# A transformer block on one core: sequence 0 in another order, ternary weights in one form, dense key-value sums

## The chip, the cores and the metric

The kernel runs on one core of a Trainium2 chip. A core has five engines that run their own instruction streams side by side: TensorE (matrix products, PE in the profile, its weight loads PEld), VectorE (DVE), ScalarE (ACT), GpSimd (POOL) and SyncE (SP, which here issues DMAs). The metric is the device time of one execution in microseconds.

## The reference

Sixteen sequences of 512 tokens with 512 features go through one pre-norm block: mLSTM attention of eight heads, then a feed-forward with ternary weights.

```python
def _mlstm_scan(q, k, v, i_pre, f_pre):          # per head, over the 512 tokens
    f_log = jax.nn.log_sigmoid(f_t)
    m_new = jnp.maximum(f_log + m, i_t)
    F = jnp.exp(f_log + m - m_new)
    I = jnp.exp(i_t - m_new)
    C_new = F[..., None, None] * C + (I[..., None] * k_t)[..., :, None] * v_t[..., None, :]
    n_new = F[..., None] * n + I[..., None] * k_t
    h_num = jnp.einsum('bhd,bhdv->bhv', qs, C_new)
    qn = jnp.einsum('bhd,bhd->bh', qs, n_new)
    h = h_num / (jnp.maximum(jnp.abs(qn), jnp.exp(-m_new)) + EPS)[..., None]

def _L0_attn_ref(x, ...):                        # q, k: 8 heads of 32; v: 8 heads of 64
    i_pre = soft_cap(x @ Wig.T + big)
    f_pre = soft_cap(x @ Wfg.T + bfg)
    h_norm = _multihead_norm(h, gamma)           # per head, over its 64 numbers
    y = (jax.nn.sigmoid(x @ Wog.T) * h_norm) @ Wout.T

def absmean_quant(w):
    scale = jnp.mean(jnp.abs(w))
    return jnp.sign(w) * (jnp.abs(w) >= scale * 0.7)

def _L0_ffn_ref(x, w1, b1, w2, b2):              # 512 -> 2048 -> 512
    h = jax.nn.gelu(x @ absmean_quant(w1).T + b1, approximate=False)
    return h @ absmean_quant(w2).T + b2

x = x + _L0_attn_ref(_layernorm(x), ...)
x = x + _L0_ffn_ref(_layernorm(x), ...)
```

## The kernel before

**Precision.** A product of two f32 matrices is made in f16 with both split into a high and a low part: high by high, low by high and high by low, three matmuls of 128 x 512 for each 128 rows of the contraction. The ternary weights are exact in f16 and need two (high and low of the activations). Small f32 products (scores times values, transposes, the state) are f32 matmuls.

**Attention by chunks.** A sequence is cut into four chunks of 128 tokens. `scores(b, g)` makes query-key products for four heads at a time, `weigh(b, n)` on VectorE multiplies those of head n with its decays (`dec`). A chunk's result is the sum of two things in the same PSUM bank: what earlier chunks left in the state, `chunk_state`, and the weighed scores times the values with a column of ones (64 + 1 = 65 columns a head), `chunk_head`. Two groups of four heads, of 32 query features each, fill the 128 rows of a product. The state before a chunk is built in two steps. `outer(b, j)` makes the key-value sum of chunk j per head, eight products of 65 columns into 32 rows of `ph`, and `state(b, j)` on VectorE adds it to the decayed previous one, densely in the free half of `kT`. Then `spread_state` on GpSimd writes it out to `cst` as a block-diagonal matrix of 4 x 65 = 260 columns (multiplied with `own_head`, a mask of each head's 32 rows), so that `chunk_state` can treat four heads in one f32 product of 128 rows and 260 columns, two products a chunk. `head_stats` on VectorE reads a chunk's result, takes its mean per head, and squares (ScalarE), a power (GpSimd) and the gate follow.

**PSUM.** There are eight banks of 512 f32 columns, in pairs: `pa` (projections and half of the scores), `pf` (feed-forward), `ps` (key transposes, the other half of the scores), `ph` (values 2 and 3, gate columns, key-value sums, chunk results). A use of a bank waits for the release of its previous use; in `pa` the uses are numbered (`U_GATE` to `U_Y`).

**Order.** No scheduler orders the work: each engine runs a program written out by hand, with semaphores between them. For sequences 1 to 15 the attention of sequence b and the feed-forward of sequence b - 1 (`fb`) are interleaved: on TensorE `hidden(...)` are first-layer tiles, `model(...)` second-layer ones, and each chunk's eight head products have one second-layer matmul between each two. After sequence 15 its feed-forward runs alone. The normalised next inputs are prepared in the same pass.

**Sequence 0** has no feed-forward beside it. In its place all weights are made ready. Five matrices are read in f32: the gates' and `Wv` first, then `Wq` with `Wk`, `Wog`, `Wout`. TensorE transposes them (`weights`), four tiles into one bank of `wbank`, ScalarE writes the high part (`weights_hi`) and VectorE the low part (`weights_lo`). `wbank` has four banks (both of `ps`, both of `pf`), used in turn. The maxima of the weights (`maxima`) are needed for scaling; `w1` and `w2` are summed in magnitude on ScalarE (`absolute_sums1`, `absolute_sums2`), `weight_sums` adds over the partitions and `thresholds` makes the ternary bounds. `w1` and `w2` are 16 units of 128 x 512 each. The units of `w1` become ternary by a comparison on GpSimd (even units) or VectorE (odd ones) and a second operation on VectorE for each; TensorE transposes two units with eight f16 transposes into one bank, and ScalarE copies 128 x 1024 out. The units of `w2` go by pairs in another form: ScalarE makes two signs of the even unit, VectorE two operations of the odd one, TensorE twelve small matmuls with the identity into two banks, ScalarE two sign copies. The `w1` pairs lie between the heads of `scores` and `weigh`; those of `w2` come through `between(...)`, between the key-value sums, the chunks and the projections of the result (`project`), after each of which VectorE has a `residual`.

Two places of the hand-written order, from TensorE's program (L1799) and from VectorE's:

```python
                key_tokens_first(b)
                for n in range(T):
                    tokens(b, U_O + n, xT[:, :, n, :, :], C_O)
                    if first and n == 1:
                        weight_sums()
                key_tokens_last(b)
                outer(b, 0)
```
```python
                between(4)
                between(5)
                residual(b, 0, ca)
                between(6)
                residual(b, 1, ca)
```

## Time and profile before

| what | value |
|---|---|
| time, median of 3 runs | 1897.43 us (1897.35 to 1898.04) |
| the profiled execution: its time / its span | 1898.05 us / 1896.3 us |
| TensorE busy | 1829.0 us, 96% |
| VectorE busy | 1231.2 us, 65% |
| ScalarE busy | 1034.1 us, 55% |
| GpSimd busy | 625.7 us, 33% |
| mean granted TensorE clock | 0.98 of full speed |

The span is what the profiler saw from the first instruction to the last; the execution's own time is 1.75 us longer. A busy share is an average over stages with different limits, so the sections below read single stretches. The clock stands as a share of 2.4 GHz: 1.00 is that level, 0.50 is 1.2 GHz, and a value between is a mix over the stretch. In the timeline a group of pipelined matmuls shows the time to the end of its last one, so neighbours overlap; distances between starts are exact.

### The profile page before, as it was taken

The page shows a single profiled execution, that of the slowest core. Times are in us where ns is not written, and L with a number is a line of the kernel's source. Part 1 is how long each engine was busy: PE and PEld are TensorE (multiplying, and loading weights), DVE is VectorE, ACT ScalarE, POOL GpSimd, SP SyncE. Part 2 cuts the span into 40 slices and gives each one's busy share as a digit, 9 for nine tenths or more (in the row PEclk, how much of TensorE's full clock was granted, in tenths as well). Part 3 has the DMA queues.
Part 4 walks back from the last instruction along what each step waited for, and adds up shares of the span by engine and source line. Part 5 has one row for each costly group of instructions (what it writes and reads, how often), then busy time and mean ns, then how long its engine had stood idle before and what let it go on. Part 6 is the DMA issues. An engine that isn't in the chain of part 4 may idle for free.

```text
span 1896.3 us, 28994 instructions
## 1 busy us (share of the span) xinstructions
PE 1829.0 (96%) x11260; PEld 966.7 (51%) x11260; DVE 1231.2 (65%) x2259; ACT 1034.1 (55%) x1711; POOL 625.7 (33%) x447
## 2 busy tenths in 40 slices
PE   5779999999999999999999999999999999999989
PEld 3364544545455464645546464554645455464544
DVE  6877575675767667575765757576575756746542
ACT  6657647274563727456372745737275473736523
POOL 1534133433414343241434324143432324333230
PEclk8769999999999999999999999999999999999989
DMA  7423224251422425042251513325141432413010
GB/s 276 161 80 96 57 71 111 51 137 25 113 51 54 134 49 139 23 115 51 51 137 45 134 32 104 62 51 137 45 124 35 103 71 51 115 42 102 12 40 22
DMA packets 233512, 156.78 MB, mean 83 GB/s; under 512 B 195088, under 2 KB 199312, under 8 KB 228256
## 3 DMA queue, kind: packets, MB, share of 16 engines
q1 hardware_dynamic: 231792, 151.79, 31.2%
q10 hardware_dynamic: 1584, 3.15, 0.5%
q8 instruction: 89, 1.46, 0.3%
q14 instruction: 47, 0.39, 0.1%
HBM read 90.48 MB, written 17.24 MB: 57 GB/s over the span
## 4 chain that ended last, share of the span: by engine, by line
PE 76%; DVE 11%; ACT 7%; issue 2%; DMA 0%; POOL 0%; SPq 0%; POOLq 0%; DVEq 0%; ACTq 0%
PE pf L1736 23%; PE pf L1722 21%; PE pa L1612 17%; PE pa L1594 5%; PE ph L1695 4%; ACT dec L855 2%; PE ph L1689 2%; ACT L875 1%; DVE g L1188 1%; DVE g L1186 1%; DVE mean L1115 1%; ACT gT L758 1%; DVE xres L1332 1%; PE ps L1671 1%; PE ph L1653 1%
## 5 line engine op out<-in xcount | busy, mean ns | idle before, releaser
L1736 PE MATMUL pf<-w2T,gT 128*128 128x512 f16 x2048 | 535.2, 379 | 0.0
L1722 PE MATMUL pf<-x2T,w1T 128*128 128x512 f16 x2048 | 457.4, 381 | 3.4 <-ACT g L875 2.8
L1348 DVE SCALAR_TENSOR_TENSOR gT<-g,wscale,gT 128x512 f16<-128x512 f32 x256 | 192.1, 750 | 205.6 <-ACT gT L878 204.2
L1722 PEld LDWEIGHTS pf<-x2T,w1T 128*128 128x128 f16 x2048 | 194.5, 98 | 237.7 <-ACT g L875 5.9
L1736 PEld LDWEIGHTS pf<-w2T,gT 128*128 128x128 f16 x2048 | 224.4, 111 | 173.8
L1612 PE MATMUL pa<-wT,xT 128*128 128x512 f16 x1152 | 256.3, 381 | 1.9 <-DVE qT L1164 1.2
L568 POOL TENSOR_TENSOR dec<-dec,causal 128x1024 f32<-128x1024 f32 x64 | 170.2, 2690 | 248.1 <-DMA dec<-gate_r 248.1
L875 ACT ACTIVATE g<-pf,b1c 128x512 f32<-128x512 f32 x256 | 175.7, 686 | 86.8 <-PE pf L1722 86.6
L883 ACT ACTIVATE ktok<-kT 128x512 f32<-128x512 f32 x64 | 40.3, 630 | 325.6 <-DVE kT L1286 325.6
L1695 PEld LDWEIGHTS ph<-vaug,dec 128*128 128x128 f32 x1024 | 184.4, 195 | 19.9
L878 ACT ACTIVATE gT<-g,wscale 128x512 f16<-128x512 f32 x256 | 184.8, 722 | 8.4
L583 POOL TENSOR_TENSOR cst<-kT,own_head 128x520 f32<-128x520 f32 x48 | 51.5, 1073 | 408.2 <-DVE kT L1242 227.1
L1612 PEld LDWEIGHTS pa<-wT,xT 128*128 128x128 f16 x1152 | 111.8, 98 | 136.4 <-DVE qT L1164 5.8
L1594 PE MATMUL pa<-xT,wT 128*128 128x512 f16 x768 | 173.0, 382 | 7.5 <-ACT kT L833 6.6
L1612 PE MATMUL pa<-wT,hoT 128*128 128x512 f16 x768 | 176.1, 383 | 0.0
L1695 PE MATMUL ph<-vaug,dec 128*128 128x65 f32 x1024 | 170.1, 253 | 0.0
L590 POOL TENSOR_TENSOR hinv<-hvar,half 128x8 f32<-128x8 f32 x64 | 105.1, 1643 | 165.3 <-DVE hvar L1299 165.3
L855 ACT ACTIVATE dec<-dec,gtok 128x128 f32<-128x128 f32 x512 | 155.8, 390 | 1.4 <-POOL dec L568 1.1
L597 POOL TENSOR_TENSOR qT<-kT,qT 128x512 f16<-128x512 f32 x64 | 74.3, 1161 | 206.5 <-ACT qT L890 206.5
L1277 DVE TENSOR_TENSOR den<-ph,gtok 128x8 f32<-128x8 f32 x64 | 10.6, 166 | 175.1 <-PE ph L1695 175.1
L1594 PEld LDWEIGHTS pa<-xT,wT 128*128 128x128 f16 x768 | 74.3, 98 | 97.2 <-ACT kT L833 8.4
L1612 PEld LDWEIGHTS pa<-wT,hoT 128*128 128x128 f16 x768 | 75.8, 99 | 91.4 <-issue 3.0
(211 smaller groups left out, 2358.4 us busy)
## 6 DMA issues: line engine op xcount, KB each, us to landing
dec<-gate_r SPq DMA_DIRECT2D x32, 1024.0 KB, 6.4
xin<-L_attn_x SPq DMA_DIRECT2D x16, 1024.0 KB, 6.1
out<-x1b SPq DMA_DIRECT2D x64, 256.0 KB, 2.2
xres<-L_attn_x SPq DMA_DIRECT2D x16, 512.0 KB, 6.1
xres<-L_attn_x SPq DMA_DIRECT2D x32, 256.0 KB, 3.6
qw<-gate_w SPq DMA_DIRECT2D x128, 48.0 KB, 5.9
gT<-L_ffn_w SPq DMA_DIRECT2D x5, 1024.0 KB, 4.9
gT<-L_ffn_w ACTq DMA_DIRECT2D x3, 1024.0 KB, 5.6
```

What stands on the lines that cost most here:

```text
L568: nc.gpsimd.tensor_tensor(rows_of, rows_of, causal[:, :].unsqueeze(1).to_broadcast([P, 2 * T, P]), ALU.add).then_inc(masked, 1)
L590: nc.gpsimd.tensor_tensor(hinv[:, :], hvar[:, :], half[:, :], ALU.pow).then_inc(pool_a, 1)
L597: nc.gpsimd.tensor_tensor(head_parts[j % 2][:, LO, :], cent[j % 2], head_parts[j % 2][:, HI, :], ALU.subtract).then_inc(ho_lo[j], 1)
L855: last = nc.scalar.activation(dec[:, h, tok(j)], dec[:, h, tok(j)], ACT.Exp, bias=gtok[:, j, ROW_C, h:h + 1])
L875: nc.scalar.activation(g32[:, f % 2, :], pf[:, use % 2, :], ACT.Gelu, bias=b1c[:, f:f + 1], scale=1.0 / X_SCALE).then_inc(pf_free[use % 2], 1)
L878: nc.scalar.activation(gT[:, HI, f, :], g32[:, f % 2, :], ACT.Copy, scale=wscale[:, W_GELU:W_GELU + 1]).then_inc(g_hi, 1)
L1348: nc.vector.scalar_tensor_tensor(gT[:, LO, f, :], g32[:, f % 2, :], wscale[:, W_GELU:W_GELU + 1], gT[:, HI, f, :], ALU.mult, ALU.subtract) ...
L1594: last = nc.tensor.matmul(bank, wT[:, ws, k, col:col + P], xT[:, xs, :, k, :], start=(k == 0 and n == 0), stop=(k == KD - 1 and n == 2))
L1612: last = nc.tensor.matmul(bank, src[:, xs, k, :], wT[:, ws, k, col:col + D], start=(k == 0 and n == 0), stop=(k == KD - 1 and n == 2))
L1695: last = nc.tensor.matmul(ph[:, g, i * VA:(i + 1) * VA], dec[:, h, tok(j)], vaug[:, j, h, :], start=(j == 0 and i == 0), stop=(i == H4 - 1 ...
L1722: last = nc.tensor.matmul(bank, w1T[:, k, tok(f)], x2T[:, part, :, k, :], start=(k == 0 and part == HI), stop=(k == KD - 1 and part == LO))
L1736: last = nc.tensor.matmul(bank, gT[:, part, f, tok(t)], w2T[:, f, :], start=(f == 0 and part == HI), stop=(f == NF - 1 and part == LO), sk ...
```

## The change

**Key-value sums and state.** `cst` holds the state densely (65 columns a group of heads), and `state` writes it there. `spread_state`, `own_head` and the semaphore between them are gone. `chunk_state` makes one product a head, of the head's 32 rows and 65 columns, and head i of either group writes into bank i, so four heads lie on four row groups and in four banks. `ps` and `ph` become two halves of one PSUM tensor `psh` of four banks. `chunk_head` writes the same banks, `head_stats` reads all four.

**Keys, values, gates, decays.** The values of tile 1 go to `ps` in place of `pa`; the last key transpose (`U_KLAST`) is gone from `pa`, all six key transposes stand together ahead of the output gates; the gate rows `gi`, `gf` lie in `sig`, no longer in `kT`. On ScalarE the evacuation of key tile 0 stands ahead of the last gate exponentials, and the last decays ahead of the output gates 2 and 3.

**Sequence 0.** The second `maxima` stand ahead of the values. `wbank` has six entries of which the query, key and output-gate weights use three in turn and `Wout` the two of `pa`. Attention up to chunk 0 comes first; sums, thresholds and all 16 pairs of ternary units follow it, all in the form that `w2` had. GpSimd has no part in them. VectorE makes pairs 11 and 12 behind residual 0, 13 and 14 behind residual 1, 15 behind residual 2, where the pairs up to 6 of 7 stood ahead of residual 1. SyncE's loads of `w2` stand between the head outputs.

```diff
-    U_GATE, U_V, U_K, U_Q, U_O, U_KLAST = 0, 1, 3, 5, 7, 11
-    U_S = U_KLAST + 1
+    U_GATE, U_V, U_K, U_Q, U_O, U_S = 0, 1, 2, 4, 6, 10
...
-        cst = sb("cst", [P, T - 1, HG, H4 * VA])
+        cst = sb("cst", [P, T - 1, HG, VA])
...
-        gi, gf = kT[0:NH, 0, :], kT[0:NH, 1, :]
+        gi, gf = sig[0:NH, 0, :], sig[0:NH, 1, :]
...
-        pa, pf, ps, ph = pb("pa"), pb("pf"), pb("ps"), pb("ph")
+        pa, pf = pb("pa"), pb("pf")
+        psh = ctx.enter_context(nc.psum_tensor("psh", [P, H4, 512], F32))
+        ps, ph = psh[:, 0:2, :], psh[:, 2:4, :]
...
-        wbank = [ps[:, 0, :], ps[:, 1, :], pf[:, 0, :], pf[:, 1, :]]
+        wbank = [ps[:, 0, :], pf[:, 0, :], pf[:, 1, :], ps[:, 1, :], pa[:, 0, :], pa[:, 1, :]]
...
-            return n % 2 if n in USES_OUT else n % 4
+            if n in USES_OUT:
+                return 4 + (n - USES_OUT[0]) % 2
+            return n if n in USES_V else (n - USE_GATE) % 3
...
-            def spread_state(b, j):
...
+            def signs(*pairs):
+
+                for p in pairs:
+                    m, q = matrix(p)
+                    act.wait_ge(s_w12[m][q // 2], 16)
+                    if p == 0:
+                        act.wait_ge(s_thr, 1)
+                    if p >= 2:
+                        act.wait_ge(s_ufill, p - 1)
+                    nc.scalar.activation(tern(2 * q), rows[:, 2 * q, :], ACT.Sign, bias=nthr[:, m:m + 1])
+                    nc.scalar.activation(low(2 * q), rows[:, 2 * q, :], ACT.Sign, bias=thr[:, m:m + 1]).then_inc(s_sign, 1)
...
                 if fb is not None:
                     tokens2_hi(fb, HALVES[0])
+                    keys(b, 0)
                 act.wait_ge(gate_dve, at(b, 4, 4))
...
-            def ternary(*units):
...
+            def ternary(*pairs):
+
+                for p in pairs:
+                    m, q = matrix(p)
+                    u = 2 * q + 1
+                    dve.wait_ge(s_w12[m][q // 2], 16)
+                    if p >= 2:
+                        dve.wait_ge(s_ufill, p - 1)
+                    nc.vector.tensor_scalar(low(u), rows[:, u, :], nthr[:, m:m + 1], None, ALU.is_le).then_inc(s_low, 1)
+                    dve.wait_ge(s_low, p + 1)
+                    nc.vector.scalar_tensor_tensor(tern(u), rows[:, u, :], thr[:, m:m + 1], low(u), ALU.is_ge,
                                                    ALU.subtract).then_inc(s_tern, 1)
...
                 if j > 0:
-                    pe.wait_ge(c_ok, at(b, T - 1, j))
                     for g in range(HG):
-                        nc.tensor.matmul(ph[:, g, 0:H4 * VA], qw[:, g, tok(j - 1)], cst[:, j - 1, g, :],
-                                         start=True, stop=False, skip_group_check=True)
+                        for h in range(H4):
+                            own = slice(h * DQ, (h + 1) * DQ)
+                            nc.tensor.matmul(psh[:, h, g * VA:(g + 1) * VA], qw[own, g, tok(j - 1)], cst[own, j - 1, g, :],
+                                             start=(g == 0), stop=False, skip_group_check=True)
...
-                last = nc.tensor.matmul(ph[:, g, i * VA:(i + 1) * VA], dec[:, h, tok(j)], vaug[:, j, h, :],
-                                        start=(j == 0 and i == 0), stop=(i == H4 - 1), skip_group_check=True)
+                last = nc.tensor.matmul(psh[:, i, g * VA:(g + 1) * VA], dec[:, h, tok(j)], vaug[:, j, h, :],
+                                        start=(j == 0 and g == 0), stop=(g == HG - 1), skip_group_check=True)
```

TensorE's program for sequence 0 is now, in calls: scores of both groups, `outer` 1 and 2, chunk 0, `weight_sums`, pairs 0 and 1, chunk 1, pairs 2 and 3, two tiles of `Wout`, chunk 2, pairs 4 and 5, the next input's first half, two tiles of `Wout`, chunk 3, pairs 6 and 7, the next input's second half, pairs 8 to 10, project 0, pairs 11 and 12, project 1, pairs 13 and 14, project 2, pair 15, project 3.

Three places in the order of instructions. **TensorE, sequence 0, values and weight transposes.** `L1497` (after: `L1462`) are weight transposes, `L1612` (`L1576`) the values, `L1594` (`L1552`) the first key product, `L1510` and `L1512` (`L1475`, `L1477`) the maxima. Before:

```order
L1497 MATMUL ps<-ident,gT 128x128 x4
L1497 MATMUL pf<-ident,gT 128x128 x4
L1612 MATMUL pa<-wT,xT 128x512 x12
L1510 MATMUL ph<-ident,peak 5x128
L1512 MATMUL ph<-cst 128x5
L1497 MATMUL pf<-ident,gT 128x128 x4
L1612 MATMUL pa<-wT,xT 128x512 x12
L1497 MATMUL ps<-ident,gT 128x128 x4
L1612 MATMUL ph<-wT,xT 128x512 x24
L1497 MATMUL ps<-ident,gT 128x128 x4
L1497 MATMUL pf<-ident,gT 128x128 x4
L1594 MATMUL pa<-xT,wT 128x512 x12
```

After:

```order
L1475 MATMUL psh<-ident,peak 5x128
L1477 MATMUL psh<-cst 128x5
L1462 MATMUL pf<-ident,gT 128x128 x8
L1576 MATMUL pa<-wT,xT 128x512 x12
L1462 MATMUL psh<-ident,gT 128x128 x4
L1576 MATMUL psh<-wT,xT 128x512 x12
L1462 MATMUL pf<-ident,gT 128x128 x4
L1576 MATMUL psh<-wT,xT 128x512 x24
L1462 MATMUL pf<-ident,gT 128x128 x4
L1462 MATMUL psh<-ident,gT 128x128 x4
L1552 MATMUL pa<-xT,wT 128x512 x12
```

The maxima moved ahead of the values. The last query-key tile (the lone `pf` row between the second and the last two values) goes into the bank of the first, behind which the last 24 value products stand.

**VectorE, the end of sequence 0.** `L1104` and `L1106` (after: `L1076`, `L1078`) make one odd ternary unit, `L1318` and `L1321` (`L1286`, `L1289`) are a residual and its statistics, `L1109` is the next input's normalisation. Before:

```order
L1104 TENSOR_SCALAR x2T<-gT,w 128x512
L1106 SCALAR_TENSOR_TENSOR x2T<-gT,w,x2T 128x512
L1104 TENSOR_SCALAR x2T<-gT,w 128x512
L1106 SCALAR_TENSOR_TENSOR x2T<-gT,w,x2T 128x512
L1318 SCALAR_TENSOR_TENSOR xres<-pa,evac,xres 128x512
L1321 BN_STATS stats<-xres 128x6
L1104 TENSOR_SCALAR x2T<-gT,w 128x512
L1106 SCALAR_TENSOR_TENSOR x2T<-gT,w,x2T 128x512
L1318 SCALAR_TENSOR_TENSOR xres<-pa,evac,xres 128x512
L1321 BN_STATS stats<-xres 128x6
```

After:

```order
L1286 SCALAR_TENSOR_TENSOR xres<-pa,evac,xres 128x512
L1289 BN_STATS stats<-xres 128x6
L1076 TENSOR_SCALAR x2T<-gT,w 128x512
L1078 SCALAR_TENSOR_TENSOR x2T<-gT,w,x2T 128x512
L1076 TENSOR_SCALAR x2T<-gT,w 128x512
L1078 SCALAR_TENSOR_TENSOR x2T<-gT,w,x2T 128x512
L1286 SCALAR_TENSOR_TENSOR xres<-pa,evac,xres 128x512
L1289 BN_STATS stats<-xres 128x6
L1109 TENSOR_SCALAR xin<-xin,mean,rstd 128x512 x4
L1076 TENSOR_SCALAR x2T<-gT,w 128x512
L1078 SCALAR_TENSOR_TENSOR x2T<-gT,w,x2T 128x512
```

Two units stand between the first residual and the second, where one stood, and five units in all are left behind the first residual, where two were.

**TensorE, a chunk of a later sequence.** `L1689` (after: `L1654`) is the state product, `L1695` (`L1660`) a head product, `L1736` (`L1701`) the second feed-forward layer. Before:

```order
L1736 MATMUL pf<-w2T,gT 128x512 x16
L1689 MATMUL ph<-cst,qw 128x260 x2
L1736 MATMUL pf<-w2T,gT 128x512
L1695 MATMUL ph<-vaug,dec 128x65
L1736 MATMUL pf<-w2T,gT 128x512
```

After:

```order
L1701 MATMUL pf<-w2T,gT 128x512 x16
L1654 MATMUL psh<-cst,qw 128x65 x8
L1701 MATMUL pf<-w2T,gT 128x512
L1660 MATMUL psh<-vaug,dec 128x65
L1701 MATMUL pf<-w2T,gT 128x512
```

Eight products of 65 columns stand where two of 260 stood; what surrounds them keeps its order.

## Rows read from the trace of the kernel before

**Rows 1.** Busy time by stretch: length, busy (instructions) by engine, TensorE clock, DMA share, GB/s.
```profile
0.00:153.00 153.00, 104.91 (x698) 68.46 (x699) 114.28 (x228) 95.66 (x161) 56.67 (x57) 0.79 0.49 163
75.00:100.00 25.00, 10.64 (x176) 8.18 (x176) 23.25 (x33) 10.30 (x16) 11.89 (x7) 0.57 0.45 143
264.00:376.00 112.00, 111.30 (x690) 58.30 (x689) 74.14 (x136) 60.99 (x101) 37.95 (x26) 1.00 0.30 80
94.00:153.00 59.00, 43.79 (x300) 33.81 (x301) 45.32 (x96) 33.94 (x53) 23.05 (x18) 0.73 0.26 75
```
**Rows 2.** Timeline of TensorE, gate products: start, length, engine, line, operation, tiles, count.
```profile
153.12 1.89 PE L1585 MATMUL pa<-xT,wgT 128*128 128x512 f16 x8
...
264.00 1.89 PE L1585 MATMUL pa<-xT,wgT 128*128 128x512 f16 x8
...
375.48 1.89 PE L1585 MATMUL pa<-xT,wgT 128*128 128x512 f16 x8
```
**Rows 3.** Waits of TensorE: what waited for whom, total us, times, longest.
```profile
PE pa L1594 <- ACT kT L833: 6.6, 13, 0.5
...
PE pf L1722 <- ACT g L875: 2.8, 15, 0.2
```
**Rows 4.** Timeline of ScalarE, sequence 0: decays, signs, sign copies.
```profile
65.01 2.43 ACT L855 ACTIVATE dec<-dec,gtok 128x128 f32<-128x128 f32 x8
...
99.47 0.71 ACT L727 ACTIVATE x2T<-gT,w 128x512 f16<-128x512 f32 x1
...
102.34 1.09 ACT L735 ACTIVATE w2T<-pf 128x512 f16<-128x512 f32 x2 [0.33 <-PE pf L1542]
```
**Rows 5.** Timeline of TensorE, sequence 1: a state product.
```profile
226.25 1.04 PE L1689 MATMUL ph<-cst,qw 128*128 128x260 f32 x4
227.12 0.38 PE L1736 MATMUL pf<-w2T,gT 128*128 128x512 f16 x1
```
**Rows 6.** Timeline of TensorE, sequence 3: transposes, key-value sums.
```profile
409.67 0.38 PE L1626 MATMUL pa<-ident,kT 128*128 128x128 f32 x2
409.99 0.43 PE L1653 MATMUL ph<-vaug,ktok 128*32 128x65 f32 x16
410.35 2.98 PE L1722 MATMUL pf<-x2T,w1T 128*128 128x512 f16 x13
```
**Rows 7.** Timeline of TensorE, sequence 0: eight head products of chunk 1.
```profile
112.91 1.90 PE L1695 MATMUL ph<-vaug,dec 128*128 128x65 f32 x16
114.65 0.22 PE L1540 MATMUL pf<-ident,x2T 128*128 128x128 f16 x1
```
**Rows 8.** Weight loads in groups: shapes, count, busy us, mean ns, idle before.
```profile
L1695 PEld LDWEIGHTS ph<-vaug,dec 128*128 128x128 f32 x1024 | 184.4, 195 | 19.9
...
L1671 PEld LDWEIGHTS ps<-hoT 32*128 32x128 f16 x768 | 22.0, 94 | 13.4 <-issue 13.4
```
**Rows 9.** Timeline of VectorE, sequence 0: gate chain, a ternary unit, a residual.
```profile
44.11 0.54 DVE L1202 TENSOR_TENSOR kT<-stack,qT 8x384 f32<-8x384 f32 x1
...
98.62 0.49 DVE L1104 TENSOR_SCALAR x2T<-gT,w 128x512 f16<-128x512 f32 x1 [0.54 <-PE pf L1530]
99.14 0.75 DVE L1106 SCALAR_TENSOR_TENSOR x2T<-gT,w,x2T 128x512 f16<-128x512 f32 x1
...
141.47 0.74 DVE L1318 SCALAR_TENSOR_TENSOR xres<-pa,evac,xres 128x512 f32<-128x512 f32 x1
```
**Rows 10.** Timeline of TensorE, sequence 0: keys, scores, projections, a ternary pair.
```profile
47.54 4.44 PE L1594 MATMUL pa<-xT,wT 128*128 128x512 f16 x12 [0.86 <-DVE wT L1067]
...
75.04 0.23 PE L1671 MATMUL ps<-hoT 32*128 32x128 f16 x2 [0.36 <-DVE ktok L1220]
...
130.64 3.88 PE L1612 MATMUL pa<-wT,hoT 128*128 128x512 f16 x12
...
144.50 0.22 PE L1540 MATMUL pf<-ident,x2T 128*128 128x128 f16 x1
...
145.17 2.75 PE L1612 MATMUL pa<-wT,hoT 128*128 128x512 f16 x12
```

521 lines of the change are left out of this document (248 added, 273 removed).

## The prediction

> **What bounds the kernel now.** I read the busy time by stage first. Where the feed-forward of one sequence runs beside attention of the next, TensorE is busy 111.30 of 112 us at the full clock, VectorE 74, ScalarE 61 [rows 1]: there only TensorE's work and its own short waits count. The gate product that opens a sequence starts at 153.12, 264.00 and 375.48 [rows 2]: a period of 110.88 or 111.48. The other stage is sequence 0, the first 153 us. TensorE is busy 105 of 153 there, at a mean granted clock of 0.79; VectorE 114, ScalarE 96 [rows 1]. That is a chain of engines that wait for each other, and its length is what has to be worked out. The feed-forward tail is untouched. So the change is two sums: 15 periods, and one prologue.
>
> **Later sequences.** (a) The wait at the second query or key product. TensorE waits 6.6 us in 13 places for a key evacuation (L833), and 2.8 us in 15 places for a gelu (L875) [rows 3]. After, the first key tile's evacuation stands ahead of the last gate exponentials on ScalarE, and the gate rows lie in `sig`, no longer in `kT`, so neither key evacuation waits for them. The periods with and without this wait differ by 0.60 us; 13 x 0.60 = 7.8. The gelu wait sits after the first scores, and the last decay pair stood between the output-gate copies and gelu in both orders; now the copies come last, 0.6 us each behind a decay that VectorE's work doesn't need before them. By my count gelu starts about 1 us earlier, since the idle time between copy and decays closes: 2.8 more. Sum (a) -10.6. If the copies of output gates 2 and 3 became late, the first scores would wait; they are needed 3.6 us (16 products) after the last one's product, and the exponentials in front of them take 2.4 [rows 4]. Cover enough, by about 1 us.
>
> (b) The state products. Before, two products of 260 columns take 226.25 to 227.12 = 0.87 us [rows 5], three times a sequence, 45 times in all. Each streams 217 ns twice. After, eight products of 32 rows x 65 columns, four of them on separate row groups and separate banks. The nearest rows: the key-value sums (L1653), eight products of 65 columns on four column groups. From 409.67 to 410.35, less two transposes of 0.11 each, they cost 0.46 us with the way into the tiled form and out of it [rows 6]. That is the low end. But their weights are 32 columns; the new ones load 128 columns in f32. Such loads are what the head products of sequence 0 wait for: 16 of them in 112.91 to 114.65, 109 ns each, though 65 columns stream in 54 (a quarter of 217) [rows 7]. Four rounds at 109 rather than 57 ns add 0.21: 0.67 us. I take 0.67, since the form of the load, not of the stream, is what it is nearest to: gain 0.20, x 45 = -9. At the low end -18. At the high end the four groups' loads come one after another, 16 x 0.109 + 0.2 = 1.94 us: +48. Loads of 32 rows take 94 ns in f16, those of 128 x 128 in f32 195 [rows 8]; the rows do not say whether four at once share a path.
>
> The Trainium skill (TensorE: Matmul & The Clock Gate, "LDWEIGHTS") says that a 32 x 128 load takes as long as a 128 x 128 one, as only columns count. It speaks against this change: K is cut to a quarter and the load stays. By it and row tiles that load side by side the sum is the 0.67 above; with whole-array streams hiding no load it would never reach 0.46. The TensorEngine Tiling page ("Key Properties") says that different tiles can load and multiply in parallel, which would rule out the high end. No run here shows it for f32 loads of row tiles.
>
> (c) Nothing else is on TensorE's path. Two transposes move ahead of the output gates, at the same price. GpSimd loses 48 spreads of 1.07 us, VectorE's head sums read four banks, the same 512 numbers: both engines have a third of each period or more free [rows 1]. I cost these at nothing; what covers them are the feed-forward's products between a chunk and the next. If VectorE's sums took longer from four banks by more than that, the next chunk would wait, three times a period.
> Sum for the later sequences: -10.6 - 9 = -20 (from -29; +38 with serial loads).
>
> **Sequence 0.** I strung each engine's new order with durations of before. The same list strung in the order of before ends at 152 where the trace has 153.1, so it may be 1 us short.
> 1. Early weights. The magnitudes now come ahead of the values, so VectorE's gate chain, which ended at 44.65 (44.11 + 0.54, [rows 9]), ends about 2.9 earlier, at 41.8. But only three banks now take the weight transposes, and the fourth query-key tile needs the low part of the first, which VectorE makes behind the gate chain, at 42.5. Values 2 and 3 are queued behind it on TensorE, ScalarE has their copies and an exponential to do before that tile's high part, and the keys wait for it. The first key product starts near 52.3, not 47.54 [rows 10]: +4.8. Of this ScalarE gives some back, since five of its absolute sums now stand behind the decays: first decay 67.0 (before 65.01, [rows 4]); four groups of 2.43 and four copies later, 78.9, the first scores: 79 (before 75.04, [rows 10]): +4.
> 2. To the thresholds. Before, the ternary work of w1 ran inside scores and decays. After: eight weighings, of the form of the residual's operation at 0.74 [rows 9], with the first scores before and the second between them, to about 88; second and third sums, 90; chunk 0 at half the clock, twice 1.74 = 3.5 [rows 7]; the sum product, some 0.8: thresholds at 94. That moves the work of eight pairs from before 94 to behind it.
> 3. Chunks. From 94 to its end, before had 45.3 us of VectorE and 33.9 of ScalarE in 59 [rows 1]. A pair of tiles now takes ScalarE two signs of 0.71 and two copies in 1.09 [rows 4], 2.2 with the 0.1 by which neighbours overlap, and VectorE 0.49 + 0.75 = 1.24 [rows 9]. Eight more pairs give ScalarE 33.9 + 17.6 = 51.5, less two copies of 1.0 of the first matrix that fell behind 94 before: 49.5. They give VectorE 45.3 + 9.9, less some 5 of weighings and ternary that fell there: 50. So neither is done before 144, if they never waited for each other. They do: heads 0 on VectorE at 96.6, sigmoid until 102.4, transposes 1 to 105, chunk 1 until 107.8, heads 1 until 109.8, output weights at 114, chunk 2 until 119, next x at 121 to 124.5, chunk 3 until 129, pair 8 at 136, pairs 9 and 10 to 145.
> 4. The end. The projection of tile 0 starts at 145 (before 130.6), and from here each step waits for the one before: VectorE makes pairs 11 and 12 only behind residual 0, which waits for projection 0, and TensorE needs pair 11 before projection 1. One round: projection 2.6 at the full clock (145.17 row, [rows 10]) to 5.2 at half; residual 1.5 with its statistics (0.74 the first of them); ternary 1.24; twelve small matmuls 0.7 (144.50 to 145.17, [rows 10]) to 1.4; copies 1.1; twelve more, 1.4; = 8.6 to 11.8. I have projection 1 at 156.5, projection 2 at 168.2 (a normalisation lies between), projection 3 at 175.6, the gates of sequence 1 at 178.
> Before, pairs stood one ahead of the residual and the whole end took 153.1 - 130.6 = 22.5 us from projection 0. So sequence 0 ends 25 us later: 178 against 153. With the clock full throughout the same list gives 166 (+13), at half 194 (+41); the granted clock was 0.57 from 75 to 100, with TensorE busy 10.6 of 25, and 1.00 where it is busy throughout [rows 1]. I let it rise in the list only behind solid stretches of products; with those instants shifted the list gave 173 to 181.
>
> **Sum.** 1898.05 (the profiled execution's own time) + 25 - 20 = 1903; it lies 0.6 above the median of the runs, so 1902.5 on that scale.
>
> **The rivals.**
> Cheap tiles, short prologue. The state products cost 0.46 and the clock stays up in half of the ternary stretch: +18 - 29 = -11, 1887. For it: the key-value sums did run four abreast. Against: the f32 load price.
> Low clock. TensorE is less than half busy from 94 on, and from 75 to 100, busy as little, it had 0.57 [rows 1]. With the list near half clock to its end, +38 - 20 = +18, 1916.
> Serial loads. Row groups share the load path: +25 + 38 = +63, 1960. It decides from 0.87 us a chunk upwards; the pace of sixteen f32 loads is the test.
> The prologue comes out even: if ScalarE and VectorE ran ahead as before, it would end near 158 and leave -15: 1882. Against it stands VectorE's order of residuals and ternary pairs, which is fixed in the code.
>
> **How the numbers follow.** My forecast 0.50; cheap tiles 0.20; low clock 0.15; serial loads 0.08; even prologue 0.07. Predicted 1902.5. The forecast's own range is 1894 to 1912. For 8 in 10 the range takes the cheap tiles at the low end and the low clock's centre: 1885 to 1917, which leaves out the serial loads, half of the even prologue and the far side of the low clock. A measurement of this kernel tells 0.2% (3.8 us) from no change. Faster than 1893.6: 0.27 from the two faster rivals, less what of them lies above, 0.24. Slower than 1901.2: 0.30 of the forecast, and 0.23 of the two slower ones: 0.50, leaving 0.26 for the same.
>
> **What would show it.** The period between gate products: 109.9 to 110.5 (111.48 before); under 109.6 means tiles at the low end, over 111.5 serial loads. The eight state products at 0.67 us with their ways in and out; no wait for a key evacuation left at the second query or key product. In sequence 0: thresholds at 94, projection 0 near 145, gates of sequence 1 near 178, VectorE's waits for projections between ternary pairs. I am wrong at the root if the gates of sequence 1 start before 165, or if a new wait at the scores or the keys shows in the later periods.

## The result

The changed kernel is slower. Its five runs gave a median of 1921.88 us (1913.13 to 1926.24), those of the kernel before 1898.04 (1897.35 to 1899.26): a ratio of 1.0122, with a 95% interval of 1.0108 to 1.0135, or 24 us. Forecast were 1902.5 and a range up to 1917. The direction was right, the size too small by 19 us, and the median lies outside the range; of the five runs only the fastest lies inside.

The profiled execution of after was its fastest, 1913.13 us with a span of 1911.3, so 15.0 longer than the span of before. Two questions follow. Where do these 15 us come from? And why do the other executions take 8 to 13 us more, when those of before differ by 2?

The first view is again the timeline of TensorE with the gate products that open sequences 1 to 4 (start, length, engine, line, operation, tiles, count); it answers to [rows 2]:

```profile
185.86 1.46 PE L1543 MATMUL pa<-xT,wgT 128*128 128x512 f16 x6
...
295.90 1.46 PE L1543 MATMUL pa<-xT,wgT 128*128 128x512 f16 x6
...
408.34 1.89 PE L1543 MATMUL pa<-xT,wgT 128*128 128x512 f16 x8
...
518.37 1.89 PE L1543 MATMUL pa<-xT,wgT 128*128 128x512 f16 x8
```

Sequence 0 ends at 185.86, not 153.12: 32.7 us later. The periods are then 110.04, 112.44 and 110.03. Twelve of the fourteen between gate products are 110.03; two, those of sequences 2 and 9, are 112.44 and 112.11. From the gates of sequence 1 to the end after needs 1911.3 - 185.86 = 1725.4, before 1896.3 - 153.12 = 1743.2: 17.7 less. So 32.7 - 17.7 = 15.0. Forecast were +25 and -20, together +5: of the 10 us by which this execution misses the forecast, 7.7 lie in sequence 0 and 2.3 behind it.

By stage, after (busy time by engine, clock last but two; compare [rows 1]):

```profile
0.00:186.00 186.00, 114.32 (x767) 75.46 (x768) 108.36 (x220) 106.33 (x185) 40.40 (x43) 0.74 0.40 134
94.00:145.00 51.00, 29.01 (x245) 26.22 (x246) 33.82 (x71) 35.13 (x58) 15.76 (x12) 0.63 0.44 136
145.00:186.00 41.00, 24.43 (x127) 13.29 (x126) 15.95 (x31) 15.71 (x26) 4.95 (x4) 0.71 0.04 12
410.00:522.00 112.00, 112.00 (x733) 57.96 (x731) 76.15 (x144) 61.56 (x102) 38.02 (x24) 1.00 0.33 80
```

From the page of after, busy time and share (before: 1829.0, 1231.2, 1034.1 and 625.7):

```profile
PE 1825.2 (95%) x11868; PEld 958.9 (50%) x11868; DVE 1228.3 (64%) x2251; ACT 1044.6 (55%) x1735; POOL 590.0 (31%) x388
```

The busy times hardly moved, but for GpSimd's, which lost the spreads and is not the bottleneck; so the 15 us are waits and clock. In the last 41 us of sequence 0 no engine is busy for more than 60% of the time: VectorE 16, ScalarE 16, TensorE 24 at a clock of 0.71. That is a chain of waits. The later sequences have no idle time left on TensorE (112.00 of 112).

### The profile page after: what moved, and what is told of

Same layout as the page of the kernel before. It is cut to its first block, busy times and chain, and to the rows that moved or that the text cites. A ratio compares the mean times of both kernels' runs of the same rounds, so it can differ in the third digit from the quotient of the medians.

```text
span 1911.3 us, 30148 instructions
## 1 busy us (share of the span) xinstructions
PE 1825.2 (95%) x11868; PEld 958.9 (50%) x11868; DVE 1228.3 (64%) x2251; ACT 1044.6 (55%) x1735; POOL 590.0 (31%) x388
## 3 DMA queue, kind: packets, MB, share of 16 engines
q10 hardware_dynamic: 1584, 3.15, 0.5%
## 4 chain that ended last, share of the span: by engine, by line
PE 89%; ACT 2%; issue 1%; POOL 1%; DVE 1%; DMA 1%; POOLq 0%; SPq 0%; DVEq 0%; ACTq 0%
PE pf L1701 23%; PE pf L1687 23%; PE pa L1576 18%; PE pa L1552 7%; PE psh L1576 6%; PE psh L1660 5%; PE psh L1654 2%; PE pa L1543 1%; POOL dec L565 1%; PE psh L1635 1%; PE psh L1617 1%; DMA dec<-gate_r 1%; PE psh L1590 0%; PE pf L1498 0%; ACT dec L839 0%
## 5 line engine op out<-in xcount | busy, mean ns | idle before, releaser
L1701 PE MATMUL pf<-w2T,gT 128*128 128x512 f16 x2048 | 535.7, 379 | 0.0
L1701 PEld LDWEIGHTS pf<-w2T,gT 128*128 128x128 f16 x2048 | 224.2, 111 | 175.6
L565 POOL TENSOR_TENSOR dec<-dec,causal 128x1024 f32<-128x1024 f32 x64 | 175.6, 2775 | 249.0 <-DMA dec<-gate_r 249.0
L1576 PE MATMUL pa<-wT,xT 128*128 128x512 f16 x960 | 213.2, 380 | 0.0
L1660 PEld LDWEIGHTS psh<-vaug,dec 128*128 128x128 f32 x1024 | 186.1, 197 | 15.3 <-DVE cst L1220 0.8
L1576 PE MATMUL pa<-wT,hoT 128*128 128x512 f16 x768 | 179.4, 388 | 0.0
L1660 PE MATMUL psh<-vaug,dec 128*128 128x65 f32 x1024 | 172.2, 256 | 0.6 <-DVE cst L1220 0.6
L1552 PE MATMUL pa<-xT,wT 128*128 128x512 f16 x768 | 171.2, 379 | 1.0 <-DVE wT L1056 1.0
L839 ACT ACTIVATE dec<-dec,gtok 128x128 f32<-128x128 f32 x512 | 154.9, 391 | 6.5 <-POOL dec L565 6.0
L1576 PEld LDWEIGHTS pa<-wT,xT 128*128 128x128 f16 x960 | 94.2, 98 | 110.0 <-issue 1.0
L1576 PE MATMUL psh<-wT,xT 128*128 128x512 f16 x576 | 129.4, 384 | 0.0
L1576 PEld LDWEIGHTS pa<-wT,hoT 128*128 128x128 f16 x768 | 76.7, 100 | 93.8 <-issue 7.3
L595 POOL TENSOR_TENSOR x1b<-xres,b2r 128x512 f32<-128x512 f32 x64 | 81.3, 1271 | 132.0 <-DVE xres L1286 95.9
L1552 PEld LDWEIGHTS pa<-xT,wT 128*128 128x128 f16 x768 | 74.4, 98 | 87.7 <-DVE wT L1056 1.2
```

The source lines that it names most:

```text
L565: nc.gpsimd.tensor_tensor(rows_of, rows_of, causal[:, :].unsqueeze(1).to_broadcast([P, 2 * T, P]), ALU.add).then_inc(masked, 1)
L595: nc.gpsimd.tensor_tensor(x1b[:, t, :], xres[:, t, :], b2r[:, :], ALU.add).then_inc(x1b_ok, 1)
L839: last = nc.scalar.activation(dec[:, h, tok(j)], dec[:, h, tok(j)], ACT.Exp, bias=gtok[:, j, ROW_C, h:h + 1])
L1552: last = nc.tensor.matmul(bank, wT[:, ws, k, col:col + P], xT[:, xs, :, k, :], start=(k == 0 and n == 0), stop=(k == KD - 1 and n == 2))
L1576: last = nc.tensor.matmul(bank, src[:, xs, k, :], wT[:, ws, k, col:col + D], start=(k == 0 and n == 0), stop=(k == KD - 1 and n == 2))
L1660: last = nc.tensor.matmul(psh[:, i, g * VA:(g + 1) * VA], dec[:, h, tok(j)], vaug[:, j, h, :], start=(j == 0 and g == 0), stop=(g == HG - ...
```

## What a later sequence gained

A state product of sequence 3, the row that answers to [rows 5]:

```profile
481.21 0.67 PE L1654 MATMUL psh<-cst,qw 32*128 32x65 f32 x16
481.82 0.39 PE L1701 MATMUL pf<-w2T,gT 128*128 128x512 f16 x1
```

Eight products take 0.61 us with their ways in and out, where two took 0.87. (Each f32 product stands in the trace as two records, so x16 are eight products.) The waits of TensorE over the whole program (us, times, longest) no longer hold one for a key evacuation; they hold these:

```profile
PE psh L1635 <- ACT sig L799: 4.7, 3, 2.4
...
PE pf L1687 <- ACT g L859: 2.3, 3, 0.9
```

The first of these is new: the first scores wait for a copy of an output gate. One of the three times, of 2.4 us, is in sequence 0; the later sequences have two, 2.3 us together. The prediction had named this wait and called the cover enough; it had also put down a new wait at the scores of the later periods as a sign that it is wrong at the root.

**Experiment: the state products twice.** It tells what four products abreast cost.

```diff
-                    for g in range(HG):
+                    for g in (0, 1, 0, 1):
                         for h in range(H4):
                             own = slice(h * DQ, (h + 1) * DQ)
```

> The changed kernel with the eight state products of a chunk issued twice (the second pass overwrites the first, so nothing else changes): 24 products more a sequence. From the profile of after, eight take 0.61 us with their ways in and out (481.21 to 481.82). If row tiles load side by side at 109 ns a round of four, eight more products are four more rounds, 0.44 us, and the period goes up 3 x 0.44 = 1.3, to 111.35. If loads come one after another and only the first was hidden: 0.61 or more each, 1.8 to 5 a period. If they are free beside the stream (54 ns a round): 0.65 a period.

Measured, two gate products of sequences 3 and 4, and one doubled state product with its successor:

```profile
414.46 1.89 PE L1543 MATMUL pa<-xT,wgT 128*128 128x512 f16 x8
...
525.84 1.89 PE L1543 MATMUL pa<-xT,wgT 128*128 128x512 f16 x8
```
```profile
487.34 1.12 PE L1654 MATMUL psh<-cst,qw 32*128 32x65 f32 x32
488.39 0.39 PE L1701 MATMUL pf<-w2T,gT 128*128 128x512 f16 x1
```

One run, 1943.35 us. The period is 111.37 in the most, 1.34 more than 110.03: 0.45 us for eight products, and 488.39 - 487.34 = 1.05 against 0.61, 0.44 more. That is four rounds of 110 ns, since 16 more records come in fours. The single records show the fours: weight loads of the doubled product start at 487.445, 487.452, 487.459 and 487.465, the next four at 487.554 to 487.574. So four f32 row tiles of 32 rows load side by side, 7 ns apart, and a round goes at the pace of one f32 load, the 109 ns of [rows 7], not at that of its 65 columns, 54 ns. Both the serial loads and the 0.46 of the key-value sums are out. The run as a whole is longer than after by more than 15 x 1.34, for two reasons beside the products: its gates of sequence 1 come at 191.72, and it has two long periods, of 113.85 and 115.28.

**Experiment: the key evacuation back behind the last gate exponentials.**

```diff
                     tokens2_hi(fb, HALVES[0])
-                    keys(b, 0)
...
-                    keys(b, 1)
+                    keys(b, 0, 1)
```

> The changed kernel with the evacuation of key tile 0 back behind the last gate exponentials in the later sequences; the gate rows stay where they are. If it was the place on ScalarE that removed the wait at the second query or key product, that wait comes back, 0.4 to 0.6 us in most sequences, and the periods are 110.5 to 110.6. If it was the gate rows' move out of the key tile, the period stays at 110.03.

Two gate products, of sequences 5 and 6, and the wait:

```profile
627.79 1.89 PE L1542 MATMUL pa<-xT,wgT 128*128 128x512 f16 x8
...
738.54 1.89 PE L1542 MATMUL pa<-xT,wgT 128*128 128x512 f16 x8
```
```profile
PE pa L1551 <- ACT kT L816: 5.9, 11, 0.6
```

One run, 1921.03 us. The wait is back in 11 places for 5.9 us, as the 6.6 in 13 places of [rows 3], and most periods are 110.74. Four are 110.08, as before had two without the wait. So the move of the gate rows out of the key tile does not remove the wait by itself; the place on ScalarE does. (Whether that place would do with the rows still in the key tile was not run.) Its price in a period is 0.66 to 0.71, somewhat over the wait itself.

## The late copies

**Why two periods are 2.1 to 2.4 longer.** ScalarE's timeline in sequence 2 (long) and in sequence 3 (normal), decays `L839`, copies `L799`:

```profile
326.74 2.44 ACT L839 ACTIVATE dec<-dec,gtok 128x128 f32<-128x128 f32 x8
331.17 2.44 ACT L839 ACTIVATE dec<-dec,gtok 128x128 f32<-128x128 f32 x8 [1.99 <-POOL dec L565]
333.52 1.24 ACT L799 ACTIVATE sig<-pa,evac 128x512 f32<-128x512 f32 x2
...
437.98 4.77 ACT L839 ACTIVATE dec<-dec,gtok 128x128 f32<-128x128 f32 x16
442.64 1.25 ACT L799 ACTIVATE sig<-pa,evac 128x512 f32<-128x512 f32 x2
```

In the long one ScalarE stands 1.99 us in front of the last decays, since GpSimd masks those (`L565`) late, and the two copies are queued behind. They start at 333.52 - 295.90 = 37.6 us of the sequence, against 34.3, and the first scores, which need their banks, wait:

```profile
335.02 0.23 PE L1635 MATMUL psh<-hoT 32*128 32x128 f16 x2 [1.31 <-ACT sig L799]
```

Before had such late masks too. In ScalarE's waits of before:

```profile
ACT dec L855 <- POOL dec L568: 1.1, 2, 0.7
```

They fell on sequences 4 and 13, whose periods are 111.49 and 111.48 like the rest: there the copies stood ahead of the decays, and nothing came of it.

**Experiment: the changed kernel once more**, for a second profile.

> The changed kernel once more, unaltered, for a second profile. Its runs spread from 1913.1 to 1926.2 us where those of before spread by 1.9. Theory A, late copies: in each later sequence in which GpSimd masks the last decays late, the two last output-gate copies come late on ScalarE and the first scores wait some 2.2 us; runs differ by how many sequences are hit (2 of 15 in the first profile, period 112.1 to 112.4 beside 110.03). A profile of an execution near 1920 then has some 6 such periods and the gates of sequence 1 near 186. Theory B, clock: runs differ in how low the clock stays in sequence 0; such a profile has its gates of sequence 1 near 194 and 2 long periods again.

Measured: 1918.81 us median (1916.54 to 1923.27); the profile had a span of 1915.7. Its gates of sequence 1 are at 186.3, and three periods are long, those of sequences 2, 9 and 13 (112.2, 112.3, 112.4). So long periods differ in number from one execution to the next, two here and three there, and in this execution the third is 2.3 of the 4.4 us; 0.4 more are in sequence 0 and 1.7 behind the gates of sequence 15. But neither theory is settled: the profile fell on an execution of 1917, with three long periods where theory A wanted six near 1920, and with its gates at 186 where theory B wanted 194.

**Experiment: both copies back ahead of the last decays.**

```diff
                 decay(b, 4)
-                decay(b, 6)
                 output_gate(b, 2, 3)
+                decay(b, 6)
```

> The changed kernel with the last two output-gate copies back ahead of the decays of heads 6 and 7 on ScalarE, in all sequences. Theory A: no period of 112 left, 15 periods of 110.0 to 110.1, the wait of the first scores for a copy gone, the runs within 2 us of each other as those of before, median about 1911.3 - 4.5 + 1.8 = 1908.6, less up to 2 in sequence 0. Theory B: the spread stays at some 10 us and the median stays above 1915. A third way: gelu starts later by the decays of two heads and the period rises to 110.2 or 110.5.

Measured: 1920.96 us (1919.33 to 1921.94), a ratio of 1.0116 (1.0099 to 1.0132) to before. The spread fell to 2.6 us, but theory A's time, 1908.6, was missed by 12: gelu pays, as the third way had it, and the gates of sequence 1 come at 187.98. The periods are 110.51, and the late masks (sequences 9 and 13) give 111.57 and 111.07. The waits for gelu:

```profile
PE pf L1687 <- ACT g L859: 8.1, 16, 1.5
```
```profile
440.96 0.67 ACT L799 ACTIVATE sig<-pa,evac 128x512 f32<-128x512 f32 x1
442.90 0.69 ACT L799 ACTIVATE sig<-pa,evac 128x512 f32<-128x512 f32 x1 [1.27 <-PE pa L1576]
443.49 2.43 ACT L839 ACTIVATE dec<-dec,gtok 128x128 f32<-128x128 f32 x8
```

ScalarE idles 1.27 us for the last product and only then turns to the decays. So beside the other steps this one gives 110.51 - 110.03 = 0.48 us in each sequence, 7 in all, and takes 2.1 to 2.4 in each with a late mask, where the old order loses 0.6 to 1.1.

A late mask can cost more than that. The kernels of the section on sequence 0 below keep this order of copies and decays, and they have periods of 113.8 to 114.5 beside such of 112.0 to 112.6. In both kinds the first mask starts 22.0 to 22.7 us into the sequence, against 20.6 to 21.4 elsewhere. In one of 114.45 (sequence 9 of the run with the fourth query-key tile behind the values) the stretch behind the wait reads (stretch, length, busy by engine, clock):

```profile
1105.00:1110.00 5.00, 4.08 (x31) 1.61 (x20) 2.50 (x4) 3.86 (x7) 0.00 (x0) 0.68 1.06 181
```

TensorE waited 1.7 us there for the copy and 0.9 for gelu, and its clock, 1.00 before, fell. Of thirteen long periods looked at in six traces, the clock fell behind the wait in all seven of +3.8 to +4.4 us and stayed at 1.00 in all six of +2.1 to +2.5, among them both of after. So such a wait costs 2 us when the clock holds and 4 when it falls. How many of the slower executions of after had such a fall was not seen.

**Experiment: copy 2, decay 6, copy 3, decay 7.**

> The changed kernel with ScalarE's order copy 2, decay of head 6, copy 3, decay of head 7 (all sequences). In the profile of after the last product of the output gates ends 33.8 us into a sequence and the first scores follow at 37.8; where the mask of heads 6 and 7 comes late (its start at 30.5 to 30.8 of the sequence, not 28.4) copy 3 starts at 38 and the scores wait. Theory: copy 3 now starts near 34 in a normal sequence and near 35.5 in a late one, gelu stays within 0.3 of its place; so all periods are 110.0 to 110.1 and no 112 is left, against 110.5 with both copies ahead: 1911.3 - 4.5 + 1.8 = 1908.6, and 1908 to 1916 with the clock of sequence 0. Rival: gelu slips by a copy's 0.6 us and periods are 110.3 or more.

Measured: 1915.11 us (1912.68 to 1917.78), 1.0092 (1.0077 to 1.0107) to before. Normal periods are 110.03, so the gain is kept; but three are still 111.8 to 112.0. The expectation that no long one is left was wrong. The median is 3.7 us below the second sample of after, 1918.81, and 6.8 below the first, 1921.88, near the spread of either. The waits say where the lateness went:

```profile
PE pf L1690 <- ACT g L860: 5.8, 4, 1.9
```

The scores no longer wait, the gelu behind them does, since it stands behind the same decays. In none of the three orders tried is the lateness of the mask hidden altogether; the order chooses what it hits.

## Where sequence 0 lost its time

The end of sequence 0 in after, TensorE (L1498 are a ternary pair's products, L1576 a projection), then VectorE. It answers to [rows 10]:

```profile
149.19 3.83 PE L1576 MATMUL pa<-wT,hoT 128*128 128x512 f16 x12
156.33 0.22 PE L1498 MATMUL pf<-ident,x2T 128*128 128x128 f16 x1 [3.31 <-issue]
158.42 0.27 PE L1498 MATMUL pf<-ident,x2T 128*128 128x128 f16 x1 [1.27 <-ACT w2T L718]
159.65 3.72 PE L1576 MATMUL pa<-wT,hoT 128*128 128x512 f16 x12
168.44 0.27 PE L1498 MATMUL pf<-ident,x2T 128*128 128x128 f16 x1 [5.07 <-issue]
171.15 0.27 PE L1498 MATMUL pf<-ident,x2T 128*128 128x128 f16 x1 [1.27 <-ACT w2T L718]
172.38 4.18 PE L1576 MATMUL pa<-wT,hoT 128*128 128x512 f16 x12
179.86 0.27 PE L1498 MATMUL pf<-ident,x2T 128*128 128x128 f16 x1 [3.30 <-issue]
181.09 4.93 PE L1576 MATMUL pa<-wT,hoT 128*128 128x512 f16 x12
```
```profile
153.06 0.75 DVE L1286 SCALAR_TENSOR_TENSOR xres<-pa,evac,xres 128x512 f32<-128x512 f32 x1 [5.21 <-PE pa L1576]
153.85 0.69 DVE L1289 BATCH_NORM_STATS2 stats<-xres 128x6 f32<-128x512 f32 x1
154.57 0.86 DVE L1076 TENSOR_SCALAR x2T<-gT,w 128x512 f16<-128x512 f32 x1
155.47 0.75 DVE L1078 SCALAR_TENSOR_TENSOR x2T<-gT,w,x2T 128x512 f16<-128x512 f32 x1
```

VectorE waits 5.21 us for projection 0, makes the residual, then the odd unit of pair 11, done at 156.2, and TensorE, idle since 153.0, takes the pair at 156.33. Three such rounds follow each other, of 10.5, 12.7 and 8.7 us.

**Experiment: units ahead of the residuals.**

```diff
-                    residual(b, 0, ca)
                     ternary(11, 12)
+                    residual(b, 0, ca)
+                    ternary(13)
                     residual(b, 1, ca)
                     norm_apply(b + 2)
-                    ternary(13, 14)
+                    ternary(14)
                     residual(b, 2, ca)
```

> The changed kernel with VectorE's odd units of pairs 11 and 12 made ahead of residual 0, pair 13 behind residual 0, 14 behind residual 1, 15 behind residual 2. Tests whether the order of residuals and units on VectorE sets the end of sequence 0. In the profile of after projection 0 starts at 149.2 and the gates of sequence 1 at 185.9, 36.7 us. If that order sets it, TensorE's pair 11 follows projection 0 at once (it waited 3.3 us) and the rounds shrink to 7, 10, 8 and 4.5: gates near 178, 7 to 9 us earlier. If ScalarE's copies or the clock set it, under 3 us come back.

```profile
148.71 3.79 PE L1577 MATMUL pa<-wT,hoT 128*128 128x512 f16 x12
154.44 0.22 PE L1499 MATMUL pf<-ident,x2T 128*128 128x128 f16 x1 [1.27 <-ACT w2T L718]
155.11 2.75 PE L1577 MATMUL pa<-wT,hoT 128*128 128x512 f16 x12
...
176.58 1.89 PE L1544 MATMUL pa<-xT,wgT 128*128 128x512 f16 x8
```

One run, 1909.10 us. Projection 0 starts 0.5 earlier, the gates 9.3 earlier, at 176.58: 8.8 us by the order of units and residuals alone, at the same clock (0.73 in after from 145 to 176, 0.74 here). The first round is 6.4 us where it was 10.5. The mechanism of this part of the prediction is confirmed.

**Experiment: the fourth query-key tile behind the values.**

```diff
                         late_values(b, t)
-                    prepare(*USES_QK[t + 2:t + 3])
+                    if t == 0:
+                        prepare(USES_QK[2])
+                prepare(USES_QK[3])
```

> The changed kernel with TensorE's transposes of the fourth query-key tile behind the values of tiles 2 and 3. In the profile of after TensorE stands 6.5 us in front of them (until 43.45), with 24 value products queued behind, and ScalarE idles 10.1 us for those. If the three banks cause the late start of the keys (53.8, before 47.5), the first key product comes at 48 to 50, first scores 4 us earlier, gates of sequence 1 at 182. If VectorE's chain sets it anyway, the keys stay near 53.

```profile
45.69 2.75 PE L1552 MATMUL pa<-xT,wT 128*128 128x512 f16 x12 [0.45 <-DVE wT L1056]
...
71.13 0.23 PE L1635 MATMUL psh<-hoT 32*128 32x128 f16 x2 [2.41 <-ACT sig L799]
```

One run, 1917.26 us. The first key product starts at 45.69, where it was 53.82 (and 47.54 in before): 8.1 earlier, more than the 4 to 6 expected. The first scores start at 71.13 instead of 79.27, 8.1 earlier, chunk 2's state product at 108.63 instead of 117.04, 8.4 earlier. Then it is given back: chunk 3's comes at 122.39 instead of 127.24, the gates of sequence 1 at 182.18, 3.7 earlier. The stretch from chunk 2's state product to chunk 3's shows why, in after first, then in this run (stretch, length, busy by engine, clock):

```profile
117.04:127.24 10.20, 6.21 (x74) 5.51 (x73) 8.37 (x18) 7.64 (x14) 2.76 (x2) 0.99 0.34 113
```
```profile
108.63:122.39 13.76, 11.03 (x73) 9.97 (x73) 9.65 (x19) 8.21 (x14) 3.85 (x3) 0.50 0.32 96
```

The same work takes 10.20 us at a clock of 0.99 and 13.76 at 0.50, 3.6 more. The kernel with both copies back ahead of the last decays has 13.75 there, also at 0.50, and the second profile of after 10.19, at 0.96. So the three banks cost 8 us up to the scores; the prediction's +4 for the whole early change holds, because the rest of that change gives 4 back (75.04 in before, 71.13 here). The gates met the expected 182 only since the clock took half of the gain.

**Experiments: all pairs in the places of before.** The same form of ternary tiles, but thresholds and pairs inside the weighings, with the absolute sums and the loads of `w2` moved ahead to suit, and units 12 and 13 ahead of residual 0. In TensorE's program (the lines that go are left out):

```diff
                     scores(b, 0)
+                    ternary_transpose(0, 1, 2, 3)
                     scores(b, 1)
+                    ternary_transpose(4, 5, 6, 7)
                     outer(b, 1)
+                    ternary_transpose(8)
                     outer(b, 2)
+                    ternary_transpose(9)
                     chunk(0, 0, 0)
...
+                    ternary_transpose(10)
...
+                    ternary_transpose(11)
                     project(b, 0)
+                    ternary_transpose(12)
                     project(b, 1)
+                    ternary_transpose(13)
                     project(b, 2)
+                    ternary_transpose(14, 15)
                     project(b, 3)
```

> The changed kernel with its ternary form, but all pairs in the places of before: thresholds behind the decays' start, one pair beside each head's weighing, pairs 8 and 9 by the second and third sums, 10 and 11 among the chunks, 12 to 15 among the projections with two made ahead of residual 0. Absolute sums stand ahead of the decays. Theory: the place costs, not the form: the eight pairs of the first matrix run at ScalarE's 2.2 to 2.4 us a pair inside the weighings, and gates of sequence 1 come at 155 to 162, of which up to 6 are the values' wait and later decays. Rival: the form costs, since ScalarE now has 2.2 us a pair more than the 1.0 of before in that stretch: gates at 168 or later.

> The same as the kernel with the pairs in the places of before, and the fourth query-key tile's transposes behind the values. Gates of sequence 1 at 151 to 158, later periods of 110.03 and some 3 of 112.3: 1911.3 - 31 + 1.8 = 1882, 1877 to 1890, faster than before by about 15 us. If the early parts overlap otherwise and nothing comes of the values' place, it equals the other kernel within 1 us in its gates of sequence 1.

The first: 1894.69 us in one run, gates of sequence 1 at 162.17. The second, with the fourth tile behind the values as well: 1883.81 us (1882.32 to 1891.74), a ratio of 0.9937 (0.9913 to 0.9960) to before, so **faster than both kernels**, by 14 us or 0.6% against before. Its gates:

```profile
151.19 1.89 PE L1538 MATMUL pa<-xT,wgT 128*128 128x512 f16 x8
```

That is 34.7 earlier than in after, with the same form of tiles: 23.7 by the place of the pairs and what was moved with them, some 9 of it the order of units and residuals, and 11.0 by the fourth tile. With the form kept, sequence 0 is as short as before, 151.19 against 153.12: the place of the pairs cost the time, not their form. ScalarE does a pair in 2.2 us beside a weighing of 0.7, and both engines have work while scores and decays run.

## The clock in sequence 0, and what spreads the runs

**Experiment: the same with the split order of copies and decays.**

> The kernel with the pairs in the places of before and the fourth query-key tile behind the values, with the same split order of copies and decays. Gates of sequence 1 at 151, all periods 110.0 to 110.1: 1882.8 - 7.2 (its three long periods, 2.0 + 2.5 + 2.5) = 1875.6; runs within 3 us of each other. If the long periods have another cause, they stay and it gives 1883.

Measured: 1884.55 us (1880.44 to 1890.26), 0.9933 (0.9918 to 0.9948) to before; no better, and 9 above the 1875.6 expected. Two periods are long, 111.6 each, and sequence 0 ended at 156.51, 5.3 later than in the kernel that differs only in where copies 2 and 3 stand (in sequence 0 too: its first pair is already 1.1 late). From 100 to 150 us TensorE's clock was (first the kernel with the pairs in the places of before, then this one; stretch, length, busy by engine, clock):

```profile
100.00:150.00 50.00, 40.52 (x261) 32.16 (x260) 37.12 (x81) 26.28 (x43) 20.69 (x16) 0.69 0.23 48
```
```profile
100.00:150.00 50.00, 40.76 (x253) 32.68 (x252) 33.19 (x76) 25.35 (x41) 19.24 (x15) 0.59 0.26 53
```

TensorE is busy for the same time and gets through less of its work. In these 50 us of interrupted work the granted clock is a mix of its two levels, 1.2 and 2.4 GHz, and the program alone does not settle the mix: the same kernel, after, has 0.64 here and in its second profile 0.60. In its slower runs the mean clock over the span is 0.965 to 0.967, where the profiled one has 0.973: 0.006 to 0.008 of 1915 us are 11.5 to 15.3 us of full clock, somewhat more than the 8 to 13 us between them, as if TensorE had bound all of it. A fall behind a late mask as in the row above takes 5 x 0.32 = 1.6 us of clock, three of them 4.8, so by this estimate more than half of it would be in sequence 0. Those runs left no trace; what part of their time is clock and what part long periods stays open.

**Experiment: the read of the gate rows first.** It asks what makes the masks late. SyncE reads the decays' rows back from memory (two transfers of 1 MB) behind the store of the other gate rows.

```diff
             def gate_rows(b):
...
-                sp.wait_ge(gate_act, at(b, 5, 4))
-                sp.dma_start(gate_w[b], ge[:, 0:LATE]).then_inc(w_stored, 16)
...
                                  .rearrange("p (h s) -> p h s", s=S)).then_inc(r_loaded[g], 16)
+                sp.wait_ge(gate_act, at(b, 5, 4))
+                sp.dma_start(gate_w[b], ge[:, 0:LATE]).then_inc(w_stored, 16)
```

> The kernel with the pairs in the places of before and the fourth query-key tile behind the values, with SyncE's read of the stored gate rows (the one that fills the decays) issued ahead of the store of the other gate rows, in all sequences. In the profile of after that read is issued 16.4 us into a sequence, both in the long periods and in the others, and GpSimd's first mask starts at 20.6 to 21.4, in the long ones at 22.1 to 22.5. Theory: the long periods come from the read landing late, so an issue 0.4 to 1.2 us earlier takes the late masks below 22 and most long periods go: 1882.8 - 5 to 7 = 1876 to 1878. Rival: the read is slowed by what shares the queues at that time and lands as late as before: three periods of 112.0 to 112.6 stay.

Measured: 1886.08 us (1885.13 to 1887.18), 0.9940 (0.9923 to 0.9956) to before. The late masks are gone: no wait for a copy of an output gate is left in any later sequence, and the runs lie within 2.1 us of each other. So the late read was the cause. But the time did not fall to the 1876 to 1878 expected: nine other periods grew, by up to 2.1 us and 7.4 in all, as much as the three long ones had cost, 7.1, and sequence 0 ended at 153.7. The waits of TensorE and of ScalarE from 400 to 1700:

```profile
PE pf L1682 <- DMA x2T<-gT: 6.2, 7, 1.6
```
```profile
ACT qT L825 <- DMA gate_w<-qT: 45.1, 11, 4.7
```

The small store now goes out behind 2 MB of reads, and ScalarE's evacuation of the queries waits for it in 11 sequences. The 45.1 us are not all new: at the same line ScalarE stood 42.9 us for TensorE's products in the kernel without this edit. The loads and transposes of SyncE behind the store come later too, down to the feed-forward's input, for which TensorE now waits. One lateness was traded for another.

## Why the prediction was right in direction and short in size

- **Later sequences, the gains: right.** Forecast -20 with a period of 109.9 to 110.5; it is 110.03, and the stretch behind the gates of sequence 1 is 17.7 shorter with two long periods in it, 22.2 without them. (b) 0.67 for the state products, measured 0.61: -11.7 in 45, not -9. (a) The key wait went, and the gelu wait outside the long periods but for 0.4 us; what the state products leave of the 22.2 is 10.5, and the forecast for (a) was 10.6. Its two parts can't be told apart: undoing either alone costs 0.5 to 0.7 a period, since each shifts ScalarE as a whole.
- **Later sequences, a step that failed:** "Cover enough, by about 1 us." I had counted the exponentials in front of the copies, 2.4 us, and not what those wait for. The trace of before had masks that came late in 2 sequences of 16. Each now costs 2.1 to 2.4, 4.5 in the first profile, 6.7 in the second, and about 4 where the clock falls behind the wait.
- **Sequence 0, the step that failed most:** "sequence 0 ends 25 us later". It ended 32.7 later (33.1 in the second profile), through steps 3 and 4 below. This is 7.7 of the 10 us of the profiled execution.
- **Steps 1 and 2: the times right.** First key product 52.3 forecast, 53.8 measured; first scores 79 and 79.27; thresholds 94 and 93.6. By the experiment the three banks cost 8 of that, and the rest of the early change gave 4 back.
- **Step 3, short by 4.** Chunk 1's state product was at 104.57 (I had chunk 1 until 107.8, it took till 109), chunk 2 at 117.0, chunk 3 at 127.2, projection 0 at 149.2 and not 145. The split of the next input waited for TensorE's transposes, eight of which took 1.9 us at half clock, and pair 8 waited 3.15 for VectorE's unit behind that split.
- **Step 4, the mechanism right, its clock too high: short by another 4.** From projection 0 to the gates it took 36.7 us, where I had 33. Rounds 10.5, 12.7 and 8.7 lie in or near 8.6 to 11.8, and the order of residuals and units is shown as their cause, 8.8 us of it. Projection 3 took 4.93 us, where I had 2.4: near half clock, up to the end. So the gates came at 185.9, outside my 173 to 181.
- **The range** had the low clock as a rival with 0.15. Sequence 0 at +32.7 and +33.1 is between the forecast's +25 and the +38 of that rival, nearer to the rival, and the runs went on from there to 1926. I had taken the spread of before, under 1 us, as that of after. That rival's premise, TensorE less than half busy from 94 on, did not hold as it stands: it was busy 29 of 51 us and 24 of 41, at clocks of 0.63 and 0.71. The other 9 us of the miss are the step from the profiled execution to the median, and no trace says what they are. What the traces do show to vary in this program are the clock of its half-busy stretch, 0.64 and 0.60, and the number of late reads, two and three.
- "The prologue comes out even" was wrong for this kernel, but it is what the version with the pairs in their old places and the fourth tile behind the values does.

## What to carry to other kernels

Work that only fills gaps (here the ternary tiles) belongs beside a chain, not behind it: its form mattered little here, its place 24 us, and 9 of them were a pair of operations on the wrong side of a residual. When an operation is moved behind another, ask what that other waits for, in its worst instance in the trace, not what it lasts. And where a stretch runs half busy at a mixed clock, price it near the low level, and do not count a gain in front of it as gained: here 8.4 us shrank to 4.8 within one chunk at 0.50.

## What was not expected of the hardware

- Four f32 products on four row groups of 32 rows and in four banks run side by side, with loads 7 ns apart, at 110 ns a round, the pace of a single f32 load of 128 columns; the 65 columns that each streams cost nothing on top. The Trainium skill (TensorE: Matmul & The Clock Gate, "LDWEIGHTS") says that a load's time goes by its columns, not its rows, and TensorEngine Tiling ("Key Properties") that tiles work in parallel. The trace of the doubled products agrees with both, now for f32 row tiles.
- Issuing one 12 KB store behind two reads of 1 MB in SyncE's program held ScalarE in 11 sequences, up to 4.7 us, and the feed-forward's transposed input came up to 1.6 us late.
- Waits of TensorE of 1.9 to 2.6 us in all, in a period that is busy throughout, cost 2.0 to 2.5 us in some periods and 3.8 to 4.4 in others; in one of the second kind the clock read 0.68 for the 5 us behind the wait, and in the first kind it stayed at 1.00. In sequence 0 the same work took 10.2 us at 0.96 to 0.99 and 13.8 at 0.50.
